# Two slots of 64 KB, x and u in one DMA each, and a tail of groups of 4, 2, 1 and 1 rows

## The chip, the cores and the metric

One NeuronCore of a Trainium2 chip runs the whole kernel. The metric is the device time of one execution in microseconds. The kernel before takes 653.01 us (median of three runs, 652.92 to 654.58).

## The reference

x is 8192 x 64, adj 8192 x 8192, u 8192 x 64, all float32.

```python
keep = (u >= 0.1).astype(x.dtype)
x_drop = x * keep / (1.0 - 0.1)
y = x + jnp.matmul(adj, x_drop)
out = (y - mean(y)) / sqrt(var(y) + 1e-5)     # over the 64 features of each row
```

adj has 268.4 MB, and each element of it is used once, against the 64 columns of x_drop.

## The kernel before

Row r of the output is row p * 64 + t, partition p, position t; a "row" of the kernel is one t, so it stands for 128 rows of the output. adj is rearranged on the host into chunks that are loaded as they lie. The output is made in groups: 7 full groups of R = 8 rows and short ones of 4, 2 and 2. For each group all 64 tiles of the contraction (KT) are multiplied: weights x_drop[:, t] (64 columns), moving data adj, the sum in PSUM `acc`. The lower half of the group's columns goes to partitions 0 to 63, the upper half to 64 to 127 (`product`, L168); a float32 product is two matmul passes in the trace, so a tile of a full group is 4 passes of 512 columns.

SP (L109) loads chunks of [128 x 8192] float32 (32 KB per partition, 4 MB) into a ring of four slots. It loads slot s again once `chunk_used` says that PE has done the chunk in it. The last chunk comes in five pieces (L124). ACT's queue (L155) loads x and u in four column pieces each; DVE (L259) waits for piece i of both and makes x_drop from it in two operations; PE waits for `drop_ready` before the tiles that need it. A chunk of a full group is 8 tiles, so two chunks use one piece.

At a group's end ACT copies acc to SBUF (L144), PE transposes it back (`turn_back`, L178), DVE adds x (L224), takes bn_stats per row (L230), combines the halves' statistics (L236 to L246), ACT takes the root (L147), DVE the reciprocal and the normalised rows (L252), and ACT's queue stores them (L152). PE goes on with the next group right after its transposes. The order on each engine is the program's; semaphores join them:

```python
with sp.Fori(1, CHUNKS // SLOTS - 1) as turn:
    for s in range(SLOTS):
        sp.wait_ge(chunk_used, (turn - 1) * SLOTS + s + 1)
        sp.dma_start(adj_ring[:, s, :], adj[turn * SLOTS + s]).then_inc(chunk_loaded[s], 16)
```

Of the kernel before, what the change touches and what calls it, by code (L numbers as in the profile page):

```python
# [26 lines left out]

assert FULL * R + sum(SHORT) == KT
assert sum(LAST_PARTS) == SLOT

SHORT_GROUPS = [(FULL * R + sum(SHORT[:n]), rows, FULL * NC + sum(SHORT[:n]) * NC // R)
                for n, rows in enumerate(SHORT)]


def build(nc: bass.Bass, x: bass.AP, adj: bass.AP, u: bass.AP, out: bass.AP):

# [11 lines left out]
    out_rows = out.rearrange("(p t) d -> p (t d)", p=P)  # L48

    with ExitStack() as ctx:  # L50
# [13 lines left out]
        identity = sb("identity", [P, P])  # L64
        eps = sb("eps", [P, 1])
# [25 lines left out]
        identity_ready = sem("identity_ready")  # L91
        acc_copied = sem("acc_copied")
# [10 lines left out]
        normed_ready = sem("normed_ready")  # L103
        out_stored = sem("out_stored")

        block = ctx.enter_context(nc.Block())

        @block.sync
        def _(sp):  # L109

            for s in range(SLOTS):
                sp.dma_start(adj_ring[:, s, :], adj[s]).then_inc(chunk_loaded[s], 16)
            with sp.Fori(1, CHUNKS // SLOTS - 1) as turn:
                for s in range(SLOTS):

                    sp.wait_ge(chunk_used, (turn - 1) * SLOTS + s + 1)
                    sp.dma_start(adj_ring[:, s, :], adj[turn * SLOTS + s]).then_inc(chunk_loaded[s], 16)  # L117

            first = CHUNKS - SLOTS
            for s in range(SLOTS - 1):  # L120
                sp.wait_ge(chunk_used, first - SLOTS + s + 1)
                sp.dma_start(adj_ring[:, s, :], adj[first + s]).then_inc(chunk_loaded[s], 16)
            sp.wait_ge(chunk_used, CHUNKS - SLOTS)
            for i, width in enumerate(LAST_PARTS):  # L124
                cols = slice(sum(LAST_PARTS[:i]), sum(LAST_PARTS[:i]) + width)
                sp.dma_start(adj_ring[:, SLOTS - 1, cols], adj[CHUNKS - 1][:, cols]).then_inc(last_loaded[i], 16)

# [7 lines left out]

        @block.scalar
        def _(act):
            def group(n, row, rows, chunks, parts):

                act.wait_ge(chunk_used, chunks)  # L140
                width = rows * P // 2 // parts
                for b in range(parts):

                    nc.scalar.copy(acc_sb[:, b * width:(b + 1) * width],  # L144
                                   acc[:, b * width:(b + 1) * width]).then_inc(acc_copied, 1)
                act.wait_ge(squares_ready, n + 1)
                nc.scalar.activation(std[:, 0:rows], squares[:, 0:rows], ACT.Sqrt, scale=1.0 / D,  # L147
                                     bias=eps[:]).then_inc(std_ready, 1)


                act.wait_ge(normed_ready, n + 1)
                act.dma_start(out_rows[:, bass.ds(row * D, rows * D)],  # L152
                              normed[:, bass.ds(row * D, rows * D)]).then_inc(out_stored, 16)

            for i in range(PIECES):  # L155
                cols = slice(i * PIECE, (i + 1) * PIECE)
                act.dma_start(x_nat[:, cols], x_rows[:, cols]).then_inc(x_loaded[i], 16)  # L157
                act.dma_start(u_nat[:, cols], u_rows[:, cols]).then_inc(x_loaded[i], 16)  # L158
            act.wait_ge(eps_ready, 1)
            with act.Fori(0, FULL) as g:  # L160
                group(g, g * R, R, (g + 1) * NC, 2)
            for n, (row, rows, chunk) in enumerate(SHORT_GROUPS):
                group(FULL + n, row, rows, chunk + rows * NC // R, 1)
            act.wait_ge(out_stored, 16 * (FULL + len(SHORT)))

        @block.tensor
        def _(pe):
            def product(rows, slot, tt, t):  # L168

# [19 lines left out]
            part_at = [sum(LAST_PARTS[:i]) for i in range(len(LAST_PARTS))]  # L189

            pe.wait_ge(identity_ready, 1)
            with pe.Fori(0, FULL) as g:
                tiles = SLOT // (R * P)
                for k in range(NC):
                    if k * tiles % PT == 0:
                        pe.wait_ge(drop_ready, k * tiles // PT + 1)

                    pe.wait_ge(chunk_loaded[k % SLOTS], (g * (NC // SLOTS) + k // SLOTS + 1) * 16)
                    for tt in range(tiles):
                        last = product(R, k % SLOTS, tt, k * tiles + tt)  # L200
                    last.then_inc(chunk_used, 1)
                turn_back(R, 2, g * 2)
            for n, (row, rows, chunk) in enumerate(SHORT_GROUPS):
                tiles = SLOT // (rows * P)
                for k in range(KT // tiles):
                    slot = (chunk + k) % SLOTS
                    final = chunk + k == CHUNKS - 1
                    if not final:
                        pe.wait_ge(chunk_loaded[slot], ((chunk + k) // SLOTS + 1) * 16)
                    for tt in range(tiles):  # L210
                        if final and tt * rows * P in part_at:
                            pe.wait_ge(last_loaded[part_at.index(tt * rows * P)], 16)
                        last = product(rows, slot, tt, k * tiles + tt)
                    last.then_inc(chunk_used, 1)
                turn_back(rows, 1, 2 * FULL + n)

        @block.vector
        def _(dve):
            def group(n, row, rows, parts, done):

                width = rows * D // parts
# [36 lines left out]

            for i in range(PIECES):  # L259
                cols = slice(i * PIECE, (i + 1) * PIECE)  # L260
                dve.wait_ge(x_loaded[i], 32)
                nc.vector.scalar_tensor_tensor(out=x_drop[:, cols], in0=u_nat[:, cols], scalar=P_DROP,  # L262
                                               in1=x_nat[:, cols], op0=ALU.is_ge, op1=ALU.mult
                                               ).then_inc(kept_ready, 1)
                dve.wait_ge(kept_ready, i + 1)
                nc.vector.tensor_scalar(x_drop[:, cols], x_drop[:, cols], 1.0 / (1.0 - P_DROP), None,  # L266
                                        ALU.mult).then_inc(drop_ready, 1)
            with dve.Fori(0, FULL) as g:
                group(g, g * R, R, 2, g * 2)
            for n, (row, rows, _) in enumerate(SHORT_GROUPS):  # L270
                group(FULL + n, row, rows, 1, 2 * FULL + n)
# [26 lines left out]
```

## Time and profile before

| | us |
|---|---|
| median of 3 runs | 653.01 |
| the profiled execution | 654.65 |
| its span, first to last instruction | 652.8 |
| PE busy | 493.9 (76%) |
| DVE busy | 45.5 |
| ACT busy | 26.4 |
| mean granted TensorE clock | 0.94 |

Busy times are sums over the span; the DMA lines say how many GB/s the core's 16 DMA engines moved in each of 40 equal slices. In a timeline a bracket holds the idle time of the engine before the line and what ended it. "DMA to landing" is the time from the issue of a transfer until it is complete.

### The profile page before, as it was taken

What the parts mean: (1) busy time and instruction counts of PE and PEld (TensorE: products, weight loads), DVE (VectorE), ACT (ScalarE), POOL (GpSimd) and SP (SyncE); (2) the same over time, 40 slices, a digit from 0 to 9 for tenths busy, and PEclk for the clock granted to TensorE, in tenths of its full rate; (3) what the DMA queues carried; (4) which work ended last, traced back from release to release, by engine and by line L of the source; (5) the groups of instructions that cost most, each with busy time, mean ns of one, the idle gap of its engine ahead of it and who ended that gap; (6) DMA issues with size and microseconds to landing.
All of it is one profiled execution on the core that took longest, in us unless ns stands there. A gap on an engine that the chain in (4) does not pass through costs nothing.

```text
span 652.8 us, 5964 instructions
## 1 busy us (share of the span) xinstructions
PE 493.9 (76%) x2592; PEld 189.4 (29%) x2592; DVE 45.5 (7%) x223; ACT 26.4 (4%) x41; POOL 0.7 (0%) x7
## 2 busy tenths in 40 slices
PE   0269569986987778886886777976878777976877
PEld 0023123322222222222222222222222222344776
DVE  0100111100020001000020000200002000020111
ACT  0000001000010001000010000200002000000000
POOL 0000000000000000000000000000000000000000
PEclk9998689999988989989989989999889989999889
DMA  8999999999999999999999999999999999999992
GB/s 357 434 434 432 434 416 443 432 424 442 426 432 428 442 420 444 432 424 442 426 430 430 440 422 442 424 434 438 430 430 437 432 420 444 424 429 438 434 409 99
DMA packets 12394, 274.87 MB, mean 421 GB/s; under 512 B 1377, under 2 KB 1761, under 8 KB 4065
## 3 DMA queue, kind: packets, MB, share of 16 engines
q1 hardware_dynamic: 9792, 268.44, 95.7%
q10 hardware_dynamic: 2592, 6.29, 2.5%
q8 instruction: 8, 0.13, 0.1%
q14 instruction: 2, 0.01, 0.0%
HBM read 272.63 MB, written 2.10 MB: 421 GB/s over the span
## 4 chain that ended last, share of the span: by engine, by line
DMA 68%; PE 23%; another core or an unknown queue 6%; DVE 1%; issue 1%; ACTq 0%; ACT 0%; SPq 0%; DVEq 0%
DMA adj_ring<-adj_chunks 61%; PE acc L173 22%; DMA u_nat<-u 7%; DVE x_drop L262 1%; DVE x_drop L266 0%; PE back L186 0%; SPq L117 0%; ACTq L157 0%; ACT acc_sb L144 0%; DVE u_nat L252 0%; ACTq L158 0%; DVE stats L230 0%; ACT std L147 0%; DVE summed L224 0%
## 5 line engine op out<-in xcount | busy, mean ns | idle before, releaser
L173 PE MATMUL acc<-adj_ring,x_drop 128*64 128x512 f32 (+2 forms) x2560 | 487.8, 540 | 149.9 <-DMA adj_ring<-adj_chunks 103.6
L173 PEld LDWEIGHTS acc<-adj_ring,x_drop 128*64 128x64 f32 x2560 | 186.1, 145 | 446.5 <-issue 320.4
L224 DVE TENSOR_TENSOR summed<-back,x_nat 128x256 f32<-128x256 f32 (+1 forms) x17 | 6.3, 405 | 512.8 <-PE back L186 512.8
L144 ACT COPY acc_sb<-acc 128x256 f32<-128x256 f32 (+1 forms) x17 | 5.4, 362 | 583.0 <-PE acc L173 583.0
L252 DVE TENSOR_SCALAR u_nat<-summed,mean,rstd 128x64 f32 (+1 forms) x64 | 15.2, 309 | 1.0
L262 DVE SCALAR_TENSOR_TENSOR x_drop<-u_nat,x_nat 128x1024 f32<-128x1024 f32 x4 | 4.9, 1225 | 87.2 <-DMA u_nat<-u 87.2
L144 ACT ACT_TABLE_LOAD x7 | 9.0, 1283 | 23.9 <-DVE u_nat L252 18.7
L186 PE MATMUL back<-identity,acc_sb 128*128 128x128 f32 x32 | 6.1, 302 | 4.5 <-ACT acc_sb L144 4.5
L230 DVE BATCH_NORM_STATS2 stats<-summed 128x6 f32<-128x64 f32 x64 | 9.0, 210 | 0.1
L147 ACT ACT_TABLE_LOAD x7 | 9.0, 1283 | 0.1
L186 PEld LDWEIGHTS back<-identity,acc_sb 128*128 128x128 f32 x32 | 3.3, 140 | 12.1 <-ACT acc_sb L144 11.6
L147 ACT ACTIVATE std<-squares,eps 128x8 f32<-128x8 f32 (+2 forms) x10 | 3.0, 300 | 16.6 <-DVE squares L246 16.6
L266 DVE TENSOR_SCALAR x_drop<-x_drop 128x1024 f32<-128x1024 f32 x4 | 2.8, 694 | 0.1
L249 DVE RECIPROCAL rstd<-std 128x8 f32<-128x8 f32 (+2 forms) x10 | 1.9, 193 | 3.7 <-ACT std L147 3.7
L236 DVE TENSOR_TENSOR gap<-stats 128x8 f32<-128x8 f32 (+2 forms) x10 | 1.7, 169 | 0.3
L244 DVE TENSOR_SCALAR mean<-twice_mean 128x8 f32<-128x8 f32 (+2 forms) x10 | 1.7, 171 | 0.0
L238 DVE TENSOR_TENSOR twice_mean<-stats 128x8 f32<-128x8 f32 (+2 forms) x10 | 1.6, 162 | 0.0
L237 DVE TENSOR_TENSOR within<-stats 128x8 f32<-128x8 f32 (+2 forms) x10 | 1.6, 162 | 0.0
L246 DVE TENSOR_TENSOR squares<-within,between 128x8 f32<-128x8 f32 (+2 forms) x10 | 1.6, 160 | 0.0
L240 DVE SCALAR_TENSOR_TENSOR between<-gap 128x8 f32<-128x8 f32 (+2 forms) x10 | 1.6, 158 | 0.0
L133 POOL TENSOR_SCALAR_AFFINE_SELECT identity<-identity 128x128 f32<-128x128 f32 x1 | 0.3, 295 | 0.2 <-POOL identity L131 0.2
L131 POOL MEMSET identity<- 128x128 f32 x1 | 0.2, 205 | 0.0
(5 smaller groups left out, 0.5 us busy)
## 6 DMA issues: line engine op xcount, KB each, us to landing
adj_ring<-adj_chunks SPq DMA_DIRECT2D x63, 4096.0 KB, 31.5
x_nat<-x ACTq DMA_DIRECT2D x4, 512.0 KB, 46.1
u_nat<-u ACTq DMA_DIRECT2D x4, 512.0 KB, 56.6
adj_ring<-adj_chunks SPq DMA_DIRECT2D x1, 2048.0 KB, 27.2
out<-u_nat ACTq DMA_DIRECT2D x7, 256.0 KB, 14.2
adj_ring<-adj_chunks SPq DMA_DIRECT2D x1, 1024.0 KB, 29.4
adj_ring<-adj_chunks SPq DMA_DIRECT2D x1, 512.0 KB, 30.2
adj_ring<-adj_chunks SPq DMA_DIRECT2D x2, 256.0 KB, 30.4
```

The source lines that it names most:

```text
L144: nc.scalar.copy(acc_sb[:, b * width:(b + 1) * width], acc[:, b * width:(b + 1) * width]).then_inc(acc_copied, 1)
L147: nc.scalar.activation(std[:, 0:rows], squares[:, 0:rows], ACT.Sqrt, scale=1.0 / D, bias=eps[:]).then_inc(std_ready, 1)
L173: last = nc.tensor.matmul(acc[h * D:(h + 1) * D, 0:width], x_drop[:, t * D:(t + 1) * D], adj_ring[:, slot, at:at + width], start=(t == 0), ...
L186: last = nc.tensor.transpose(back[b][:, c * P:(c + 1) * P], acc_sb[:, at:at + P], identity[:])
L224: nc.vector.tensor_tensor(summed[:, b * width:(b + 1) * width], back[b][:, 0:width], x_nat[:, bass.ds(row * D + b * width, width)], ALU.ad ...
L230: last = nc.vector.bn_stats(stats[:, r, :], summed[:, r * D:(r + 1) * D])
L236: nc.vector.tensor_tensor(gap[:, 0:rows], m0, m1, ALU.subtract).then_inc(gap_ready, 1)
L244: nc.vector.tensor_scalar(mean[:, 0:rows], twice_mean[:, 0:rows], 0.5, None, ALU.mult)
L249: nc.vector.reciprocal(rstd[:, 0:rows], std[:, 0:rows]).then_inc(rstd_ready, 1)
L252: last = nc.vector.tensor_scalar(normed[:, bass.ds((row + r) * D, D)], summed[:, r * D:(r + 1) * D], mean[:, r:r + 1], rstd[:, r:r + 1], A ...
L262: nc.vector.scalar_tensor_tensor(out=x_drop[:, cols], in0=u_nat[:, cols], scalar=P_DROP, in1=x_nat[:, cols], op0=ALU.is_ge, op1=ALU.mult). ...
L266: nc.vector.tensor_scalar(x_drop[:, cols], x_drop[:, cols], 1.0 / (1.0 - P_DROP), None, ALU.mult).then_inc(drop_ready, 1)
```

## The change

The main loop loads [128 x 16384] (64 KB per partition, 8 MB, 16 tiles) into two slots, and the seven full groups are 28 such chunks. x and u are loaded whole, by one DMA each; x_drop is still made in four parts. The short groups become 4, 2, 1 and 1 rows; their loads are pieces of 2 MB and 1 MB and, in the last group, of 16, 16, 8, 8, 6, 4, 3, 2 and 1 tiles of 64 KB. A group of one row has no second half: even tiles of the contraction add up in partitions 0 to 63 and odd ones in 64 to 127, and a product with `twofold` (two identities above one another) adds the two and turns them back. In the last group x is added by a product with the identity into PSUM tile `final`, and bn_stats, bn_aggr and the normalising work straight from PSUM. The tail's groups have PSUM tiles of their own, and their transposes stand behind the first piece of the next group. The copies out of PSUM move from ACT to DVE. The ring is one flat buffer, with one count `adj_used` of pieces done.

```diff
-SHORT = [4, 2, 2]
-SLOT = 8192
-SLOTS = 4
-LAST_PARTS = [4096, 2048, 1024, 512, 512]
+SLOT = 16384
+SLOTS = 2
+MAIN = FULL * NC
+RING = SLOTS * SLOT
+TAIL = [(4, [8] * 8), (2, [16, 16, 8, 8, 8, 8]), (1, [16] * 4), (1, [16, 16, 8, 8, 6, 4, 3, 2, 1])]
+WIDE = TAIL[0][1][0] * TAIL[0][0] * P
...
@@ sync
+            with sp.Fori(1, MAIN // SLOTS) as turn:
                 for s in range(SLOTS):
+                    sp.wait_ge(adj_used, (turn - 1) * SLOTS + s + 1)
+                    sp.dma_start(adj_ring[:, s * SLOT:(s + 1) * SLOT],
+                                 adj_main[turn * SLOTS + s]).then_inc(chunk_loaded[s], 16)
+            for i, (_, _, start, width, at) in enumerate(pieces(0)):
+                sp.wait_ge(adj_used, MAIN - SLOTS + at // SLOT + 1)
+                sp.dma_start(adj_ring[:, at:at + width], tail_block(start, width)).then_inc(piece_loaded[0][i], 16)
+            for n in range(1, len(TAIL)):
+                for i, (_, _, start, width, at) in enumerate(pieces(n)):
+                    sp.wait_ge(adj_used, MAIN + (at + width - 1) // WIDE + 1)
+                    sp.dma_start(adj_ring[:, at:at + width], tail_block(start, width)).then_inc(piece_loaded[n][i], 16)
@@ scalar
-            for i in range(PIECES):
-                cols = slice(i * PIECE, (i + 1) * PIECE)
-                act.dma_start(x_nat[:, cols], x_rows[:, cols]).then_inc(x_loaded[i], 16)
-                act.dma_start(u_nat[:, cols], u_rows[:, cols]).then_inc(x_loaded[i], 16)
+            act.dma_start(x_nat[:], x_rows).then_inc(x_loaded, 16)
+            act.dma_start(u_nat[:], u_rows).then_inc(x_loaded, 16)
@@ tensor
+            def product_of_one(into, at, t):
+                h = t % 2
+                return nc.tensor.matmul(into[h * D:(h + 1) * D, 0:P], x_drop[:, t * D:(t + 1) * D],
+                                        adj_ring[:, at:at + P], start=(t < 2), stop=(t >= KT - 2))
...
+                    if i == 0 and n in (1, 2):
+                        turn_back(TAIL[n - 1][0], 1, 2 * FULL + n - 1)
+                    if i == 0 and n == 3:
+                        pe.wait_ge(acc_copied, 2 * FULL + 3)
+                        pe.wait_ge(twofold_ready, 1)
+                        nc.tensor.matmul(back[0][:, 0:D], acc_sb[:, 0:P], twofold[:],
+                                         start=True, stop=True).then_inc(back_ready, 1)
+                    if i == 1 and n == 3:
+                        row = FIRST_ROW[LAST]
+                        nc.tensor.matmul(final[:], identity[:], x_nat[:, row * D:(row + 1) * D], start=True, stop=False)
+            pe.wait_ge(acc_copied, 2 * FULL + 4)
+            nc.tensor.matmul(final[:], acc_sb[:, 0:P], twofold[:], start=False, stop=True).then_inc(final_ready, 1)
@@ vector
+            def take(into, rows, used, parts):
+                dve.wait_ge(adj_used, used)
+                width = max(rows, 2) * P // 2 // parts
+                for b in range(parts):
+                    nc.vector.tensor_copy(acc_sb[:, b * width:(b + 1) * width],
+                                          into[:, b * width:(b + 1) * width]).then_inc(acc_copied, 1)
...
-                dve.wait_ge(x_loaded[i], 32)
+            dve.wait_ge(x_loaded, 32)
...
+            take(last_acc, 1, MAIN + FIRST_PIECE[LAST] + len(TAIL[LAST][1]), 1)
+            dve.wait_ge(final_ready, 1)
+            nc.vector.bn_stats(stats[:, 0, :], final[:]).then_inc(final_stats, 1)
+            dve.wait_ge(final_stats, 1)
+            nc.vector.bn_aggr(mean_var[:], stats[:, 0, :]).then_inc(final_var, 1)
+            dve.wait_ge(std_ready, FULL + LAST + 1)
+            nc.vector.reciprocal(rstd[:, 0:1], std[:, 0:1]).then_inc(rstd_ready, 1)
+            dve.wait_ge(rstd_ready, FULL + LAST + 1)
+            row = FIRST_ROW[LAST]
+            nc.vector.tensor_scalar(normed[:, row * D:(row + 1) * D], final[:], mean_var[:, 0:1], rstd[:, 0:1],
+                                    ALU.subtract, ALU.mult).then_inc(normed_ready, 1)
```

## Rows read from the trace of the kernel before

**Rows 1.** The page: the span, GB/s in 40 slices, DMA totals

```profile
span 652.8 us, 5964 instructions
...
GB/s 357 434 434 432 434 416 443 432 424 442 426 432 428 442 420 444 432 424 442 426 430 430 440 422 442 424 434 438 430 430 437 432 420 444 424 429 438 434 409 99
DMA packets 12394, 274.87 MB, mean 421 GB/s; under 512 B 1377, under 2 KB 1761, under 8 KB 4065
```

**Rows 2.** DMA queues of the page: packets, MB, share of 16 engines

```profile
q1 hardware_dynamic: 9792, 268.44, 95.7%
q10 hardware_dynamic: 2592, 6.29, 2.5%
```

**Rows 3.** Stretches: us, busy by engine, granted clock, DMA share, GB/s

```profile
0.00:5.00 5.00, 0.00 (x0) 0.00 (x0) 0.00 (x0) 0.00 (x0) 0.74 (x7) 1.00 0.66 223
...
5.00:605.00 600.00, 456.59 (x2038) 155.26 (x2040) 38.93 (x183) 24.59 (x35) 0.00 (x0) 0.94 1.00 431
...
50.00:55.00 5.00, 5.00 (x14) 1.31 (x15) 0.00 (x0) 0.00 (x0) 0.00 (x0) 0.50 0.91 385
...
640.00:642.00 2.00, 2.00 (x42) 2.00 (x40) 0.00 (x0) 0.00 (x0) 0.00 (x0) 1.00 0.24 92
```

**Rows 4.** Chain of waits: start us, us, what

```profile
364.98 31.45 DMA adj_ring<-adj_chunks
...
631.72 15.88 PE acc L173 x256
```

**Rows 5.** Lines L126 (last pieces' loads) and L152 (stores): duration ns, starts, landing

```profile
L126 SPq DMA_DIRECT2D adj_ring<-adj_chunks x5: 328/432/434, 609.4 to 611.2; - x5
...
DMA to landing us min/median/max: 27.2/30.2/30.5
...
DMA to landing us min/median/max: 1.6/14.2/15.4
```

**Rows 6.** Timeline of 0 to 100 us: start us, us, engine, line

```profile
25.77 1.23 DVE L262 SCALAR_TENSOR_TENSOR x_drop<-u_nat,x_nat 128x1024 f32<-128x1024 f32 x1 [25.77 <-DMA u_nat<-u]
...
27.87 15.70 PE L173 MATMUL acc<-adj_ring,x_drop 128*64 128x512 f32 x64 [27.87 <-DVE x_drop L266]
...
36.89 53.73 SPq L117 DMA_DIRECT2D adj_ring<-adj_chunks  x6
...
47.81 1.23 DVE L262 SCALAR_TENSOR_TENSOR x_drop<-u_nat,x_nat 128x1024 f32<-128x1024 f32 x1 [20.08 <-DMA u_nat<-u]
...
73.16 16.94 PE L173 MATMUL acc<-adj_ring,x_drop 128*64 128x512 f32 x64 [6.68 <-DVE x_drop L266]
...
93.07 1.22 DVE L262 SCALAR_TENSOR_TENSOR x_drop<-u_nat,x_nat 128x1024 f32<-128x1024 f32 x1 [20.04 <-DMA u_nat<-u]
```

**Rows 7.** Timeline of PE, 111 to 500 us

```profile
112.66 27.69 PE L173 MATMUL acc<-adj_ring,x_drop 128*64 128x512 f32 x128 [0.17 <-issue]
...
201.09 8.78 PE L173 MATMUL acc<-adj_ring,x_drop 128*64 128x512 f32 x32 [3.13 <-DMA adj_ring<-adj_chunks]
...
357.71 7.09 PE L173 MATMUL acc<-adj_ring,x_drop 128*64 128x512 f32 x32 [3.20 <-DMA adj_ring<-adj_chunks]
```

**Rows 8.** Timeline of the end, from 647 us

```profile
647.62 0.27 ACT L144 COPY acc_sb<-acc 128x128 f32<-128x128 f32 x1 [16.11 <-PE acc L173]
...
647.94 0.33 PE L186 MATMUL back<-identity,acc_sb 128*128 128x128 f32 x1 [0.36 <-ACT acc_sb L144]
...
648.70 0.35 DVE L230 BATCH_NORM_STATS2 stats<-summed 128x6 f32<-128x64 f32 x2
...
649.69 0.30 ACT L147 ACTIVATE std<-squares,eps 128x2 f32<-128x2 f32 x1 [1.80 <-DVE squares L246]
650.02 0.17 DVE L249 RECIPROCAL rstd<-std 128x2 f32<-128x2 f32 x1 [0.36 <-ACT std L147]
650.23 0.54 DVE L252 TENSOR_SCALAR u_nat<-summed,mean,rstd 128x64 f32<-128x64 f32 x2
650.80 0.35 ACTq L152 DMA_DIRECT2D out<-u_nat  x1
```

More of the change, by code:

```diff
@@ L16, with pieces @@
 FULL = 7
-SHORT = [4, 2, 2]
-SLOT = 8192
-SLOTS = 4
-CHUNKS = KT * KT * P // SLOT
+SLOT = 16384
+SLOTS = 2
 NC = KT * R * P // SLOT
-LAST_PARTS = [4096, 2048, 1024, 512, 512]
-PIECES = 4
-PT = KT // PIECES
-PIECE = PT * D
-HALF = R * P // 2
[L28 to L32, printed above, removed]
+MAIN = FULL * NC
+RING = SLOTS * SLOT
+TAIL = [(4, [8] * 8), (2, [16, 16, 8, 8, 8, 8]), (1, [16] * 4), (1, [16, 16, 8, 8, 6, 4, 3, 2, 1])]
+FIRST_ROW = [FULL * R + sum(rows for rows, _ in TAIL[:n]) for n in range(len(TAIL))]
+FIRST_PIECE = [sum(len(tiles) for _, tiles in TAIL[:n]) for n in range(len(TAIL))]
+WIDE = TAIL[0][1][0] * TAIL[0][0] * P
+X_PARTS = 4
+PART = KT * D // X_PARTS
+PT = KT // X_PARTS
+HALF = R * P // 2
+assert FULL * R + sum(rows for rows, _ in TAIL) == KT
+assert all(sum(tiles) == KT for _, tiles in TAIL)
+assert MAIN % SLOTS == 0 and len(TAIL[0][1]) * WIDE == RING
+def pieces(n):
+    rows, tiles = TAIL[n]
+    at = sum(TAIL[m][0] for m in range(n)) * KT * P
+    out = []
+    for i, count in enumerate(tiles):
+        before = sum(tiles[:i])
+        out.append((before, count, at + before * rows * P, count * rows * P, (at + before * rows * P) % RING))
+    return out
 def build(nc: bass.Bass, x: bass.AP, adj: bass.AP, u: bass.AP, out: bass.AP):
@@ L48, in build, with tail_block @@
     out_rows = out.rearrange("(p t) d -> p (t d)", p=P)
+    adj_main = adj[0:MAIN * P * SLOT].rearrange("(n p c) -> n p c", p=P, c=SLOT)
+    def tail_block(start, width):
+        first = (MAIN * SLOT + start) * P
+        return adj[first:first + width * P].rearrange("(p c) -> p c", p=P)
     with ExitStack() as ctx:
@@ L64, in build @@
         identity = sb("identity", [P, P])
+        twofold = sb("twofold", [P, D])
         eps = sb("eps", [P, 1])
@@ L111, in _ @@
             for s in range(SLOTS):
-                sp.dma_start(adj_ring[:, s, :], adj[s]).then_inc(chunk_loaded[s], 16)
-            with sp.Fori(1, CHUNKS // SLOTS - 1) as turn:
+                sp.dma_start(adj_ring[:, s * SLOT:(s + 1) * SLOT], adj_main[s]).then_inc(chunk_loaded[s], 16)
+            with sp.Fori(1, MAIN // SLOTS) as turn:
                 for s in range(SLOTS):
[L116 to L126, printed above, removed]
+                    sp.wait_ge(adj_used, (turn - 1) * SLOTS + s + 1)
[8 more added lines that the diff above has]
+                    sp.dma_start(adj_ring[:, at:at + width], tail_block(start, width)).then_inc(piece_loaded[n][i], 16)
         @block.gpsimd
@@ L134, in _, with root @@
                                     base=0, pattern=[[-1, P]], channel_multiplier=1).then_inc(identity_ready, 1)
+            pool.wait_ge(identity_ready, 1)
+            nc.gpsimd.tensor_tensor(twofold[:], identity[:, 0:D], identity[:, D:P], ALU.add).then_inc(twofold_ready, 1)
         @block.scalar
         def _(act):
[L138 to L145, printed above, removed]
+            def root(n, rows):
                 act.wait_ge(squares_ready, n + 1)
@@ L148, in group, with store @@
                                      bias=eps[:]).then_inc(std_ready, 1)
+            def store(n, row, rows):
                 act.wait_ge(normed_ready, n + 1)
@@ L196, in _ @@
                         pe.wait_ge(drop_ready, k * tiles // PT + 1)
[L198 removed]
+                    s = k % SLOTS
+                    pe.wait_ge(chunk_loaded[s], (g * (NC // SLOTS) + k // SLOTS + 1) * 16)
                     for tt in range(tiles):
[L200 to L201 removed]
+                        last = product(acc, R, s * SLOT + tt * R * P, k * tiles + tt)
@@ L202, in _ @@
+                    last.then_inc(adj_used, 1)
                 turn_back(R, 2, g * 2)
[L203 to L215, printed above, removed]
+            for n, (rows, _) in enumerate(TAIL):
+                into = tail_acc[n] if n < LAST else last_acc
+                for i, (before, count, _, _, at) in enumerate(pieces(n)):
+                    pe.wait_ge(piece_loaded[n][i], 16)
+                    for tt in range(count):
+                        if rows > 1:
+                            last = product(into, rows, at + tt * rows * P, before + tt)
+                        else:
+                            last = product_of_one(into, at + tt * P, before + tt)
+                    last.then_inc(adj_used, 1)
+                    if i == 0 and n in (1, 2):
[8 more added lines that the diff above has]
+                        nc.tensor.matmul(final[:], identity[:], x_nat[:, row * D:(row + 1) * D], start=True, stop=False)
@@ L221, in group, with normalise @@
+            def normalise(n, row, rows, parts, done):
                 width = rows * D // parts
@@ L256, in group @@
                 dve.wait_ge(normed_ready, n + 1)
-            for i in range(PIECES):
-                cols = slice(i * PIECE, (i + 1) * PIECE)
-                dve.wait_ge(x_loaded[i], 32)
+            dve.wait_ge(x_loaded, 32)
+            for i in range(X_PARTS):
+                cols = slice(i * PART, (i + 1) * PART)
                 nc.vector.scalar_tensor_tensor(out=x_drop[:, cols], in0=u_nat[:, cols], scalar=P_DROP,
@@ L268, in _ @@
             with dve.Fori(0, FULL) as g:
-                group(g, g * R, R, 2, g * 2)
-            for n, (row, rows, _) in enumerate(SHORT_GROUPS):
-                group(FULL + n, row, rows, 1, 2 * FULL + n)
+                take(acc, R, (g + 1) * NC, 2)
+                normalise(g, g * R, R, 2, g * 2)
+            for n in range(LAST):
+                take(tail_acc[n], TAIL[n][0], MAIN + FIRST_PIECE[n] + len(TAIL[n][1]), 1)
+                normalise(FULL + n, FIRST_ROW[n], TAIL[n][0], 1, 2 * FULL + n)
+            take(last_acc, 1, MAIN + FIRST_PIECE[LAST] + len(TAIL[LAST][1]), 1)
[9 more added lines that the diff above has]
+                                    ALU.subtract, ALU.mult).then_inc(normed_ready, 1)
 def kernel(x, adj, L0_gnn_u):
@@ L279 @@
     x, adj, u = np.asarray(x), np.asarray(adj), np.asarray(L0_gnn_u)
-    chunks = np.empty((CHUNKS, P, SLOT), adj.dtype)
-    by_row = adj.reshape(P, KT, N)
-    groups = [(g * R, R, g * NC) for g in range(FULL)] + SHORT_GROUPS
-    for row, rows, first in groups:
-        tiles = SLOT // (rows * P)
-        n = KT // tiles
-        part = by_row[:, row:row + rows].reshape(P, rows // 2, 2, P, n, tiles).transpose(4, 3, 5, 2, 1, 0)
-        chunks[first:first + n].reshape(n, P, tiles, 2, rows // 2, P)[...] = part
-    arrays = {"x": x, "adj_chunks": chunks, "u": u}
+    by_row = adj.reshape(P, KT, P, KT)
+    blocks = np.empty(N * N, adj.dtype)
+    tiles = SLOT // (R * P)
+    for g in range(FULL):
+        part = by_row[:, g * R:(g + 1) * R].reshape(P, R // 2, 2, P, NC, tiles).transpose(4, 3, 5, 2, 1, 0)
+        blocks[g * NC * P * SLOT:(g + 1) * NC * P * SLOT].reshape(part.shape)[...] = part
+    for n, (rows, _) in enumerate(TAIL):
+        h = 2 if rows > 1 else 1
+        group = by_row[:, FIRST_ROW[n]:FIRST_ROW[n] + rows].reshape(P, rows // h, h, P, KT).transpose(3, 4, 2, 1, 0)
+        for before, count, start, width, _ in pieces(n):
+            first = (MAIN * SLOT + start) * P
+            part = group[:, before:before + count]
+            blocks[first:first + width * P].reshape(part.shape)[...] = part
+    arrays = {"x": x, "adj_blocks": blocks, "u": u}
     nc = bacc.Bacc("TRN2", target_bir_lowering=False, num_devices=1)
```

46 lines of the change are left out of this document (30 added, 16 removed).

## The prediction

> **What bounds the kernel now.** I read the page first. The cores' 16 DMA engines move 431 to 433 GB/s in nearly every slice, from the second to the last but one, and between 5 and 605 us the mean is 431 GB/s with the engines' share at 1.00, while PE has idle time [rows 1, 3]. Almost all bytes are adj on SP's queue; x, u and the output are 6.3 MB on ACT's queue [rows 2]. So the kernel is a stream of 274.9 MB with two ends: before it flows, and after it stops. The chain of waits, read second, says the same: it goes round a loop of one 4 MB load, 31.45 us from issue to landing, and one chunk's products, 7.09 us [rows 4, 7]. Four slots at 38.8 us a loop are 9.7 us a chunk, and 4.19 MB at 431 GB/s are 9.73 us: the loop runs at the stream's pace, and most of the 31.45 us is waiting behind other loads, a reserve. Whatever leaves the DMA engines without a queued load is lost for good; whatever only PE, DVE or ACT do inside the stream is free. Third, the stretches at the end: the stream is nearly out in 640 to 642 us (92 GB/s) [rows 3], the last piece, issued at about 611.2, lands 30.2 us later, at 641.4 [rows 5], but PE works until 647.6, because the last group's 256 matmul passes run as one block from 631.72 [rows 4]; then come copy, transpose, sum, statistics, root and store, and the span ends at 652.8 [rows 8]. The end is 11.4 us behind the last landing.
>
> **Part 1, x and u in one DMA each, beside two slots of 64 KB.** Here I expect the loss. How do ACT's and SP's queues share an engine? The page counts 9792 packets on q1 [rows 2]: 63 loads with 128 rows of 32 KB, the last chunk's 5 x 128, and 68 DMAs x 16 small ones, which makes 9792 exactly, so one partition's row is one packet. The pieces of x and u have rows of 4 KB, 8 of x and 8 of u on each of 16 engines. DVE starts on the first piece at 25.77 and on the second at 47.81; there are four, evenly spaced, to 93.07 [rows 6]. If the two queues take turns packet by packet, 16 turns of 32 + 4 KB on 16 engines are 9.44 MB, at 431 GB/s 21.9 us; the rows show 22.0. By bytes in equal shares it would have been 1.05 MB of x, u and as much of adj, 4.9 us. Turns it is.
>
> Afterwards a row of x is 16 KB, a row of adj 64 KB, and there are 8 + 8 rows of either per engine before anything can be freed: the two slots hold 16 rows of 64 KB per engine. 16 turns of 80 KB on 16 engines are 20.97 MB, which is the whole ring and all of x and u. So x and u are complete only when there is nothing left to load. In time: the first 5 us carry 223 GB/s, 1.1 MB [rows 3]; the other 19.86 MB need 46.1 us; the engines run dry at 51.1. For the check, the same working gives 24.3 us for the present first piece, and DVE started at 25.77, so 1.5 us lie between last byte and use: 52.6. From DVE's start to PE's first matmul are 2.1 us (27.87 - 25.77), since x_drop still comes in quarters [rows 6]: 54.7. The first slot is 16 tiles, 64 passes of 512 columns. Before, just such blocks took 15.70 to 16.94 us after a long rest [rows 6]; I take 15.7: 70.4. Only then does SP refill slot 0. Issue to first byte isn't shown by itself: it is above 0, and below the 1.6 us in which the shortest store is issued and landed [rows 5]. I take 0.8 with SP's wait: data flow at 71.3. **The DMA engines stand idle for 20.2 us** (18.7 to 22.5 with the bounds). Before, the ring of four was first refilled at 36.89 [rows 6], while 16.8 MB of adj weren't in yet, and never ran dry. The fewer DMA instructions on ACT's queue (8 become 2) save nothing on this path. Nothing gives it back, as the stream is the bound to the end.
>
> **Part 2, the steady loop of two slots.** A slot's round is: its products, SP's wake and issue, the load. 8.39 MB are 19.46 us, so a round may last 38.9. Products: 14.0 us at full clock, 2.4 GHz (128 passes back to back took 27.69), and a start at 1.2 GHz costs 8.78 against 7.09 for 4 MB, 1.7 us more; both kinds follow rests of 3.1 to 3.2 us [rows 7]. (In 50 to 55 us, after a rest of 6 us, the granted clock is 0.50 [rows 3].) PE would now rest 19.46 - 15.7, some 3.7 us, so I take the slow start, 15.7 us, with 14.0 and 16.94 as ends. Wake and release are 0.2. What a load takes beyond its bytes is between 1.6 us (the shortest store whole) and 3.1 (1.5 of landing plus the 1.6). Sums: 14.0 + 0.2 + 19.46 + 1.6 = 35.3 at best, 16.94 + 0.2 + 19.46 + 3.1 = 39.7 at worst, in the middle 37.7. So it fits by about 1.2 us where there were some 20 us in reserve. The 13 further rounds cost 0 to 13 x 0.8 = 10 us; I take 1 us, for the first ones, which follow long rests. The evacuation at a group's end, now on DVE, and the transposes (0.8 us of copies, 0.7 of PE, by the nearest rows) begin after the slot is given back, in PE's rest of some 3.7 us; at no cost, and uncovered 1.5 us a group. DVE's next group is 78 us away. The ACT table loads that fall away are off the path.
>
> The Trainium skill ("DMA: Bandwidth & Descriptors", 🔬 Anatomy of one DMA) puts a DMA's fixed cost at about 2.0 us beside its bytes at 436 GB/s, mostly completion. As an estimate from that page a round would be 15.7 + 0.2 + 19.3 + 2.0 = 37.2 us, and the loop would hold too; no row here isolates it.
>
> **Part 3, the tail.** SP's tail loads wait only for regions whose products run earlier, up to 16.8 MB ahead, so they stay queued. In bytes nothing changes. More and shorter rows (down to 512 B; before, 2 KB was the shortest of adj) cost the stream 0 to 1 us; I take 0.3. The gain is that the last landing leaves one tile: two passes and what is left of the tile pairs before. PE's pace is enough: a row's 64 tiles are 128 passes of 128 columns in 9.7 us, while before 256 such passes took 15.88 [rows 4], 7.9 per 128. I take 0.4 us from the last landing to PE's end (0.2 if it is waiting, 3 if it meets the end at half clock with a piece behind), against 6.2. Then the chain: before, 647.60 to the store's issue at 650.80 is 3.2 us. Now: a copy on DVE of 128 columns (nearest row: ACT's 0.27; 0.2 to 0.3, take 0.25), one product of 64 columns (0.33 for the 128 column transpose, take 0.30), one bn_stats (0.21 by the two in 0.35), bn_aggr (not shown; 0.16 to 0.30, take 0.2), root 0.30, reciprocal 0.17, one tensor_scalar out of PSUM (0.54 for two, take 0.27) and 8 hand-overs of 0.04 as seen in the rows: 2.0 us [rows 8]. Store to the end 2.0 as before (652.8 - 650.8). So the end is 4.4 us behind the last landing instead of 11.4: **7.0 us won** (4 to 7.5).
>
> **The sum**, on the profiled execution (span 652.8, time 654.65): 20.2 + 1.0 + 0.3 - 7.0 = +14.5 us, so span 667.3 and time 669.2. The median of the runs shown, 653.01, lies 1.6 under the profiled one, so I forecast 667.5.
>
> **Rivals.**
> A. *x and u land early.* Mechanism: ACT's queue gets a larger share beside rows of 64 KB, in equal bytes or because a long row goes in two packets of 32 KB. Place: the first 50 us. The point that decides: DMA stays busy if u lands before 51.1 - 2.1 - 15.7 - 0.8 = 32.5 us. In equal bytes 8.4 MB are due, and u is in by 5 + 16.9 + 1.5 = 23.4; with 32 KB packets 16 turns of 48 KB, 12.6 MB, and in at 33.1: idle 0.6 us. Then the time is 653.0 + 0 to 0.6 + 1.3 - 7.0 = 647.3 to 648, with a bad loop up to 655. For it: no row of 64 KB is in the trace. Against it: 32 KB rows went whole, and the spacing of 22.0 us rules out equal bytes at that size. Chance 0.12. The Trainium skill ("DMA: Bandwidth & Descriptors", 🔬 SWDGE vs HWDGE vs iDMA) calls a packet of at most 4096 B, preferably, the boundary where an engine switches; by that rule this rival would hold. The trace disagrees with it for this queue: 22.0 us, not 4.9.
>
> B. *The loop of two starves.* PE at half clock for longer, or engines that finish a load unevenly, with nothing behind them: 0.3 to 0.8 us a chunk, 26 chunks, 8 to 20 us on top of the forecast: 675 to 687. For it: 1.2 us of reserve, and blocks of 16.94 us. Against it: a starved loop gives PE no more work, and the present rate stays within 431 to 433. Chance 0.13.
>
> C. *The tail doesn't shorten* (PE ends behind the last piece as before, by the many small matmuls and weights): 3 to 6 us more, 671 to 674. Chance 0.08.
>
> **Chances and range.** Forecast 0.67, A 0.12, B 0.13, C 0.08. From A at 647 to 655: faster 0.09, same 0.02, slower 0.01; all others are slower. Beyond 0.3% (2 us, about what can be told from no change): faster 0.09, same 0.03, slower 0.88. The range 662 to 678 leaves out A and the upper part of B.
>
> **What would show it.** In the page's slices: a hole in the DMA row of some 20 us near 51 to 71 us and none before it; DVE's first x_drop near 52.6; SP's third load issued near 70.4. In 100 to 560 us: 431 GB/s and loads of about 23 us from issue to landing; a mean under 427 means B. At the end: PE finished within 0.5 us of the last landing, and 4.4 us to the end. The forecast is wrong if DVE starts before 33 us, or if the queue share of ACT's rows isn't one row a turn.

## The result: 685.2 us, slower by 4.7%

| | us | ratio to before | 95% interval |
|---|---|---|---|
| before (4 runs beside it) | 653.80 | | |
| changed | 685.23 (680.8 to 685.99) | 1.0467 | 1.0418 to 1.0515 |

The forecast was 667.5 us with a range of 662 to 678: the sign was right, the loss 31.4 us instead of 14.5, and the time lies above the range. The profiled execution took 685.4 us, its span 683.6. Executions of the kernel before fall near 653.1 or near 654.7 us, which is why its median differs a little from one set of runs to another (653.01 and 653.80, and 653.06 to 653.16 in the experiments).

In what follows PE is the matmul engine, DVE the vector engine, ACT the scalar engine; SP's and ACT's queues issue the transfers, and all of them are carried by the same 16 DMA engines. The trace has a record for each row (one partition's part of a transfer) with its start and duration; figures said to be from the rows' records come from there.

The slices of the page after, as in [rows 1], the DMA row ahead of GB/s:

```profile
DMA  9990899999999999999999999999999999999996
GB/s 374 454 399 0 369 429 427 429 433 406 403 429 385 428 426 433 429 432 404 410 418 429 440 404 410 426 414 399 426 429 426 430 402 422 402 415 402 424 420 244
DMA packets 9801, 274.87 MB, mean 402 GB/s; under 512 B 1344, under 2 KB 1984, under 8 KB 3392
```

Two things are to be seen: a slice of 17 us in which nothing at all moves, and then a stream that keeps falling to 385 to 415, where before hardly a slice was under 420. The bytes are the same. The start, from the timelines of DVE, PE and SP after (answering to [rows 6]):

```profile
52.02 1.23 DVE L303 SCALAR_TENSOR_TENSOR x_drop<-u_nat,x_nat 128x1024 f32<-128x1024 f32 x1 [52.02 <-DMA u_nat<-u]
...
54.12 29.98 PE L197 MATMUL acc<-adj_ring,x_drop 128*64 128x512 f32 x128 [54.12 <-DVE x_drop L307]
...
70.56 502.07 SPq L142 DMA_DIRECT2D adj_ring<-adj_blocks  x26
```

Forecast were 52.6, 54.7 and 70.4. In the rows' records the last data of x, u and the first two slots end at 51.4 us and the next row of adj starts at 71.5: a hole of 20.1 us, where 20.2 were forecast. The records show the turns too. From 4.9 us on, 16 rows of ACT's queue start, one for each engine, then 16 of SP's, sixteen times over, 3.0 us a turn. The queues' packets between 10.8 and 13.8 us (q1 is SP's, q10 ACT's):

```profile
q1 hardware_dynamic: 16, 1.05, 80.6%
q10 hardware_dynamic: 16, 0.26, 20.4%
```

This excludes a rival that the times of u alone leave open: if the queues took turns load by load, eight rows an engine at once, u would be in at the same time.

The stretches (columns as in [rows 3]) show the hole, and then the loop:

```profile
50.00:70.00 20.00, 15.88 (x64) 5.21 (x66) 7.40 (x8) 0.00 (x0) 0.00 (x0) 1.00 0.03 13
...
100.00:560.00 460.00, 365.12 (x1482) 121.36 (x1480) 31.30 (x162) 9.50 (x12) 0.00 (x0) 0.88 0.99 420
```

420 GB/s over 460 us instead of 431 to 432. The engines' busy share is 0.99 all the same. The chain of waits goes round this loop (as [rows 4], two slots now):

```profile
314.67 15.66 PE acc L197 x64
330.36 0.05 SPq L142
330.50 23.82 DMA adj_ring<-adj_blocks
...
394.80 16.59 PE acc L197 x64
411.40 0.05 SPq L142
411.55 23.43 DMA adj_ring<-adj_blocks
```

A load's median from issue to landing is 24.2 us, the median block of products 15.7. The end, answering to [rows 8]:

```profile
675.69 3.71 PE L205 MATMUL tail_acc<-adj_ring,x_drop 128*64 128x128 f32 x64
679.54 0.29 DVE L259 COPY acc_sb<-tail_acc 128x128 f32<-128x128 f32 x1 [4.35 <-PE tail_acc L205]
...
679.89 0.43 PE L251 MATMUL final<-twofold,acc_sb 128*128 128x64 f32 x2 [0.49 <-DVE acc_sb L259]
680.36 0.23 DVE L318 BATCH_NORM_STATS2 stats<-final 128x6 f32<-128x64 f32 x1 [0.53 <-PE final L251]
680.63 0.18 DVE L320 BATCH_NORM_AGGREGATE mean_var<-stats 128x2 f32<-128x6 f32 x1
680.84 0.29 ACT L187 ACTIVATE std<-mean_var,eps 128x1 f32<-128x1 f32 x1 [6.20 <-DVE mean_var L320]
...
681.37 0.34 DVE L325 TENSOR_SCALAR u_nat<-final,mean_var,rstd 128x64 f32<-128x64 f32 x1
681.75 0.35 ACTq L174 DMA_DIRECT2D out<-u_nat  x1
```

The tail has 27 loads; the last is issued at 663.3 and lands 15.2 us later, at 678.5. From there PE takes 0.9 us, the chain 2.35 to the store's issue, the store 1.85 to the end of the span: 5.1 us, where it was 11.4.

### The profile page after: what moved, and what is told of

The parts are those of the page before. It is cut to its first block, busy times and chain, and to the rows that moved or that the text cites. A ratio compares the mean times of both kernels' runs of the same rounds, so it can differ in the third digit from the quotient of the medians.

```text
span 683.6 us, 5863 instructions
## 1 busy us (share of the span) xinstructions
PE 508.5 (74%) x2597; PEld 196.1 (29%) x2597; DVE 52.3 (8%) x243; ACT 12.3 (2%) x18; POOL 1.1 (0%) x8
## 4 chain that ended last, share of the span: by engine, by line
DMA 54%; PE 37%; another core or an unknown queue 8%; DVE 1%; issue 1%; SPq 0%; ACT 0%; DVEq 0%
DMA adj_ring<-adj_blocks 54%; PE acc L197 35%; PE tail_acc L197 1%; PE tail_acc L205 1%; DVE x_drop L303 0%; SPq L142 0%; PE back L213 0%; DVE acc_sb L259 0%; DVE x_drop L307 0%; PE final L251 0%; PE final L249 0%; DVE u_nat L325 0%; ACT std L187 0%; DVE stats L318 0%
## 5 line engine op out<-in xcount | busy, mean ns | idle before, releaser
L197 PE MATMUL acc<-adj_ring,x_drop 128*64 128x512 f32 x1792 | 443.0, 658 | 161.7 <-DMA adj_ring<-adj_blocks 107.6
L197 PEld LDWEIGHTS acc<-adj_ring,x_drop 128*64 128x64 f32 x1792 | 146.1, 151 | 453.9 <-issue 398.4
L197 PE MATMUL tail_acc<-adj_ring,x_drop 128*64 128x256 f32 (+1 forms) x512 | 42.9, 327 | 3.3 <-DMA adj_ring<-adj_blocks 3.3
L259 DVE COPY acc_sb<-acc 128x256 f32<-128x256 f32 x14 | 5.3, 419 | 516.5 <-PE acc L197 516.5
L197 PEld LDWEIGHTS tail_acc<-adj_ring,x_drop 128*64 128x64 f32 x512 | 32.1, 137 | 14.1 <-DMA adj_ring<-adj_blocks 5.0
L205 PE MATMUL tail_acc<-adj_ring,x_drop 128*64 128x128 f32 x256 | 15.5, 275 | 2.7 <-DMA adj_ring<-adj_blocks 2.7
L205 PEld LDWEIGHTS tail_acc<-adj_ring,x_drop 128*64 128x64 f32 x256 | 13.8, 137 | 4.0 <-DMA adj_ring<-adj_blocks 4.0
L169 ACT ACTIVATE std<-squares,eps 128x8 f32<-128x8 f32 (+3 forms) x10 | 3.0, 299 | 642.3 <-DVE squares L288 642.3
L266 DVE TENSOR_TENSOR summed<-back,x_nat 128x256 f32<-128x256 f32 (+2 forms) x17 | 6.2, 400 | 12.1 <-PE back L213 9.5
L291 DVE RECIPROCAL rstd<-std 128x8 f32<-128x8 f32 (+3 forms) x10 | 1.9, 193 | 3.7 <-ACT std L169 3.7
L278 DVE TENSOR_TENSOR gap<-stats 128x8 f32<-128x8 f32 (+3 forms) x10 | 1.7, 169 | 0.3
## 6 DMA issues: line engine op xcount, KB each, us to landing
adj_ring<-adj_blocks SPq DMA_DIRECT2D x28, 24.2
adj_ring<-adj_blocks SPq DMA_DIRECT2D x1, 384.0 KB, 22.2
```

Of the source, the lines that this page charges most:

```text
L197: last = nc.tensor.matmul(into[h * D:(h + 1) * D, 0:width], x_drop[:, t * D:(t + 1) * D], adj_ring[:, at + h * width:at + (h + 1) * width] ...
L205: return nc.tensor.matmul(into[h * D:(h + 1) * D, 0:P], x_drop[:, t * D:(t + 1) * D], adj_ring[:, at:at + P], start=(t < 2), stop=(t >= KT ...
L259: nc.vector.tensor_copy(acc_sb[:, b * width:(b + 1) * width], into[:, b * width:(b + 1) * width]).then_inc(acc_copied, 1)
L266: nc.vector.tensor_tensor(summed[:, b * width:(b + 1) * width], back[b][:, 0:width], x_nat[:, bass.ds(row * D + b * width, width)], ALU.ad ...
L278: nc.vector.tensor_tensor(gap[:, 0:rows], m0, m1, ALU.subtract).then_inc(gap_ready, 1)
L291: nc.vector.reciprocal(rstd[:, 0:rows], std[:, 0:rows]).then_inc(rstd_ready, 1)
```

## The experiments

Each ratio is to the kernel before on the same chip.

### 1. Four slots of 32 KB, the rest as changed

```diff
-SLOT = 16384
-SLOTS = 2
+SLOT = 8192
+SLOTS = 4
```

> The changed kernel with its main loop put back to four slots of 32 KB rows; x and u stay in one DMA each, the tail stays. My theory: all of the loss is in the two slots, 20 us at the start and 16 to 17 us in the loop, and the tail gains. Taking turns row by row, u is in after 16 turns of 48 KB, near 33 us, the ring isn't dry before 51, so no hole in the DMA row; 431 GB/s in 100 to 560 us; time 653.8 - 7 + 1.2 = 648 us. Rival (the new tail or the single DMAs lose by themselves): 655 us or more, with a hole before 60 us or an end as long as before.

Measured: 649.51 us, ratio 0.9945 (0.9928 to 0.9961); run again beside experiment 10: 649.55, 0.9944 (0.9930 to 0.9958). Its timelines and stretch:

```profile
33.14 1.23 DVE L303 SCALAR_TENSOR_TENSOR x_drop<-u_nat,x_nat 128x1024 f32<-128x1024 f32 x1 [33.14 <-DMA u_nat<-u]
...
43.85 487.42 SPq L142 DMA_DIRECT2D adj_ring<-adj_blocks  x52
...
100.00:560.00 460.00, 361.94 (x1522) 117.49 (x1524) 31.08 (x162) 9.50 (x12) 0.00 (x0) 0.94 1.00 432
```

DVE starts at the forecast 33, no slice is empty, the rate is 432. So the whole loss of the change, 35.7 us beside this kernel, comes with the size and number of the slots, and the new tail is a gain: 3.6 us, less than the 5.8 expected here.

### 2. Slot 1's first load behind x and u

```diff
-            for s in range(SLOTS):
-                sp.dma_start(adj_ring[:, s * SLOT:(s + 1) * SLOT], adj_main[s]).then_inc(chunk_loaded[s], 16)
+            sp.dma_start(adj_ring[:, 0:SLOT], adj_main[0]).then_inc(chunk_loaded[0], 16)
...
             act.dma_start(u_nat[:], u_rows).then_inc(x_loaded, 16)
+            act.dma_start(adj_ring[:, SLOT:2 * SLOT], adj_main[1]).then_inc(chunk_loaded[1], 16)
```

> The changed kernel, with the first load of slot 1 issued on ACT's queue behind x and u instead of on SP's queue. If the queues take turns row by row, SP's queue has only 8 rows per engine beside x and u, so u is in after 12.6 MB, near 33 us, PE starts near 35 and gives slot 0 back near 51, when the ring is just dry: the hole of 20 us shrinks to under 2 us, and the time is 685 - 19.6 = 665.6 us. If the shares go by something else (bytes, or a priority of SP's queue), the start moves little and the time stays above 675.

Measured: 665.28 us, 1.0207 (1.0159 to 1.0254). Same slots, same bytes, another order of two loads:

```profile
32.39 1.22 DVE L303 SCALAR_TENSOR_TENSOR x_drop<-u_nat,x_nat 128x1024 f32<-128x1024 f32 x1 [32.39 <-DMA u_nat<-u]
...
50.37 504.39 SPq L141 DMA_DIRECT2D adj_ring<-adj_blocks  x26
...
50.00:70.00 20.00, 14.14 (x66) 5.41 (x64) 0.00 (x0) 0.00 (x0) 0.00 (x0) 0.97 1.00 417
100.00:560.00 460.00, 366.43 (x1490) 121.59 (x1488) 31.34 (x162) 9.50 (x12) 0.00 (x0) 0.89 0.99 419
```

The hole is gone and 20.0 us are back in the median (four runs, 663.6 to 670.4); the loop is as slow as it was. The start's loss is shown by itself.

### 3. x and u in four pieces beside slots of 64 KB

```diff
-            act.dma_start(x_nat[:], x_rows).then_inc(x_loaded, 16)
-            act.dma_start(u_nat[:], u_rows).then_inc(x_loaded, 16)
+            for i in range(X_PARTS):
+                cols = slice(i * PART, (i + 1) * PART)
+                act.dma_start(x_nat[:, cols], x_rows[:, cols]).then_inc(x_loaded[i], 16)
+                act.dma_start(u_nat[:, cols], u_rows[:, cols]).then_inc(x_loaded[i], 16)
```

> The changed kernel with x and u in four column pieces each, as before; slots of 64 KB stay. Theory of turns (a row a turn): the first pieces still need 16 turns, now of 64 + 4 KB, 17.8 MB, so DVE starts near 45 us instead of 52, PE near 47.4, slot 0 is given back near 63, and only 7 us come back: 685.2 - 7 = 678 us. Rival (it is the single DMA of x and u that makes the hole, as the change's text would have it): DVE starts near 26, no hole, 665 us.

Measured: 674.42 us, 1.0302 (1.0266 to 1.0337). DVE starts at 45.14 (forecast 45), SP refills at 63.50 (63). The turns hold again; the time is 3.6 us better than worked out, within the 5 us by which runs of a two-slot loop differ among themselves (670.5 to 675.9 here).

### 4. The kernel before with x and u in one DMA each

The same edit the other way round, in the kernel before.

> The kernel before with x and u in one DMA each and nothing else changed: 16 turns of 32 + 16 KB, u in near 33 us, PE's first chunk done near 44, ring dry only at 51, so no hole and the same time as before, 653 us within 0.3%. If the single DMA costs by itself, 655 us or more.

Measured: 652.68 us, 0.9986 (0.9975 to 0.9997): the same within 0.3%. DVE starts at 33.55, PE at 35.65, SP refills at 44.25. The single DMAs cost nothing; the 16 rows of 64 KB per engine beside them do.

### 5. Rows of 32 KB in slots of 64 KB

```diff
-                sp.dma_start(adj_ring[:, s * SLOT:(s + 1) * SLOT], adj_main[s]).then_inc(chunk_loaded[s], 16)
+                for h in range(2):
+                    sp.dma_start(adj_ring[:, s * SLOT + h * SLOT // 2:s * SLOT + (h + 1) * SLOT // 2],
+                                 adj_main[s][:, h * SLOT // 2:(h + 1) * SLOT // 2]).then_inc(chunk_loaded[s], 16)
```

(and in the loop likewise, with PE waiting for 32 a turn)

> The changed kernel, each slot of 64 KB loaded by two DMAs with rows of 32 KB; a slot is still released whole. Theory R (the loop loses because a slot is given back too late, only some 1 to 2 us before the other is in): the mean in 100 to 560 us stays near 418 GB/s; the start is mended by the shorter rows (u in near 33 us, idle under 2 us), so 685 - 19.6 = 666 us. Theory P (rows of 64 KB themselves make the loop slow): 431 GB/s and about 649 us.

Measured: 668.85 us (663.74 to 670.22), 1.0248 (1.0228 to 1.0268).

```profile
100.00:560.00 460.00, 364.88 (x1498) 121.91 (x1496) 31.34 (x162) 9.50 (x12) 0.00 (x0) 0.89 0.99 421
```

Theory R, as far as the rate goes: rows of 32 KB don't mend the loop. The traced execution is the fastest of the four, and the median lies 2.9 us above the forecast of 666.

### 6 and 7. Fewer products per slot

```diff
-                    for tt in range(tiles):
+                    for tt in range(0, tiles, 2):
```

This is experiment 6; experiment 7 has `range(tiles - 2)`. In both, the `stop` of the sum moves to the last product that is left. Both kernels leave out products and so don't compute the reference; they serve to time the loop.

> The changed kernel without the products of every second tile in the main loop, so the sum of the seven full groups is incomplete; a slot is given back after some 8 us instead of 16, loads unchanged. At the start the hole shrinks by 7.8 us either way. Theory R (late release): 431 GB/s in 100 to 560 us, 685 - 7.8 - 16.5 = 661 us. Theory P (rows of 64 KB are slow by themselves): near 418 GB/s and 677 us.

> The changed kernel without the products of the last two of each slot's 16 tiles in the main loop (the sum of the seven full groups is incomplete): a slot is given back some 2 us earlier, with about 6 us instead of 4 to the other slot's landing. Start: 2 us less. Theory of late release with a threshold of some 5 us: the loop is back at 431 GB/s, so 685.2 - 2 - 16 = 667 us. If each microsecond of PE's work counted in proportion (8 us less gave 12 GB/s): near 423 GB/s, 679 us.

Measured: with half of them 661.59 us, 1.0130 (1.0113 to 1.0147); with 14 of 16 tiles 668.94 us, 1.0234 (1.0217 to 1.0251). The stretches, first of half, then of 14 tiles:

```profile
100.00:560.00 460.00, 222.16 (x772) 69.45 (x774) 31.34 (x162) 9.50 (x12) 0.00 (x0) 0.72 1.00 432
```

```profile
100.00:560.00 460.00, 341.43 (x1338) 110.66 (x1334) 31.34 (x162) 9.50 (x12) 0.00 (x0) 0.85 1.00 432
```

With rows of 64 KB and two slots untouched, two tiles fewer bring back the full rate, and leaving out six more changes nothing further. There is a threshold. It isn't PE's work as such that slows the loads: with four slots PE does all the products and the rate is 432 (experiment 1). The threshold is read off PE's timeline, where the bracket, PE's rest, is the time from handing a slot back (and issuing its load) to the landing of the other slot. Three turns of the changed kernel, then three with 14 tiles:

```profile
476.53 16.66 PE L197 MATMUL acc<-adj_ring,x_drop 128*64 128x512 f32 x64 [6.03 <-DMA adj_ring<-adj_blocks]
496.32 15.31 PE L197 MATMUL acc<-adj_ring,x_drop 128*64 128x512 f32 x64 [3.13 <-DMA adj_ring<-adj_blocks]
516.17 15.63 PE L197 MATMUL acc<-adj_ring,x_drop 128*64 128x512 f32 x64 [4.53 <-DMA adj_ring<-adj_blocks]
```

```profile
130.11 15.15 PE L197 MATMUL acc<-adj_ring,x_drop 128*64 128x512 f32 x56 [3.48 <-DMA adj_ring<-adj_blocks]
150.04 13.72 PE L197 MATMUL acc<-adj_ring,x_drop 128*64 128x512 f32 x56 [4.79 <-DMA adj_ring<-adj_blocks]
169.41 14.28 PE L197 MATMUL acc<-adj_ring,x_drop 128*64 128x512 f32 x56 [5.64 <-DMA adj_ring<-adj_blocks]
```

Where a group ends, the transposes stand inside the rest, so it is longer than the bracket: at 130.11 it is 4.8 us in all. The distance of two starts is here that of two landings. Over 24 turns of the 14-tile kernel: after a rest of 4.5 us or less (5 turns) the load issued before it lands 20.0 to 20.5 us after the other one, after 4.7 us or more (19 turns) in 19.2 to 19.5, with one of 19.9. The pace of the full stream is 8.39 MB at 432 GB/s, 19.4. In the changed kernel the median rest is 4.2 us and the landings are 20.1 us apart in the mean, up to 22.3 and 21.5 after the shortest rests of 2.8 and 3.0. So the 14-tile kernel keeps the stream full if a load is issued some 4.7 us before the other one lands. In the changed kernel the single turns scatter more (six with a rest of 4.6 us or more are followed by 19.6 to 20.1), so 4.7 us is a figure of about that size, and not a sharp limit for every loop.

### 8. Eight slots of 16 KB

As experiment 1, with SLOT = 4096 and SLOTS = 8.

> The changed kernel with eight slots of 16 KB rows in the main loop, the same 128 KB ring. 16 turns of 32 KB: u in near 23.4 us, no hole, 431 GB/s; PE's rests fall to about 1.3 us, so the granted clock rises over 0.95, off the path. Time as with four slots, 649.5 us. If more and shorter loads cost by themselves, 651 us or more.

Measured: 653.35 us, 0.9999 (0.9989 to 1.0008). The forecast of 649.5 missed; the alternative named, 651 or more, came.

```profile
23.05 1.23 DVE L303 SCALAR_TENSOR_TENSOR x_drop<-u_nat,x_nat 128x1024 f32<-128x1024 f32 x1 [23.05 <-DMA u_nat<-u]
...
100.00:560.00 460.00, 344.99 (x1516) 103.41 (x1512) 28.25 (x145) 9.50 (x12) 0.00 (x0) 1.00 1.01 429
```

The start is as worked out (23.4), and with rests of some 1.2 us the granted clock is 1.00, which helps nothing. The rate is 429 with the engines' share at 1.01: rows of 16 KB move more slowly at full load. The rows' records say it of the single row: one of 16 KB takes 614 ns, one of 32 KB (experiment 1) 1216 and one of 64 KB (the changed kernel) 2418, in the median, which is 26.7, 26.95 and 27.1 GB/s for an engine. As an estimate from the rounded rates, 235 MB of the main loop at 429 instead of 432 GB/s are 3.8 us, about the whole difference to four slots.

### 9 and 10. Longer loads in the tail

```diff
-TAIL = [(4, [8] * 8), (2, [16, 16, 8, 8, 8, 8]), (1, [16] * 4), (1, [16, 16, 8, 8, 6, 4, 3, 2, 1])]
+TAIL = [(4, [16] * 4), (2, [32, 32]), (1, [32, 32]), (1, [16, 16, 8, 8, 6, 4, 3, 2, 1])]
-                    if i == 1 and n == 3:
+                    if i == 0 and n == 3:
```

> Four slots of 32 KB rows with the new tail, its loads made longer: groups of 4 and 2 rows in rows of 32 KB (4 x 16 tiles, 2 x 32 tiles), the first group of one row in 2 x 32 tiles; and the product that adds x to the last row moved one piece earlier. If short rows are what slows the stream in the tail (431 GB/s at 32 KB, 421 in 600 to 620 us with 8 KB), 25 MB at 431 instead of some 425 save 0.9 us and the product 0.4: 648.2 us, 1.3 under the four slots with the short pieces. Rival: the rate falls for another reason (the end of the ring, the stores), and nothing changes: 649.5.

> The kernel with four slots of 32 KB rows and the new tail once more, beside the one with the longer loads, for the difference of the two: 649.5 us.

Measured: 650.37 us, 0.9961 (0.9947 to 0.9975), against 649.55, 0.9944. The stretch from 600 us of the long loads, then of the short ones:

```profile
600.00:620.00 20.00, 14.90 (x176) 12.29 (x178) 0.42 (x1) 0.00 (x0) 0.00 (x0) 0.91 1.00 428
```

```profile
600.00:620.00 20.00, 16.37 (x242) 13.66 (x240) 3.20 (x17) 0.30 (x1) 0.00 (x0) 1.00 1.00 420
```

The stream did get faster, 428 against 420, and its last load lands at 642.2 instead of 642.5. But PE, which now gets 4 MB at a time, falls behind: in the long version it hardly rests from 621.93 on and ends at 644.26, 1.0 us later than in the short one (643.28). The gain expected in the stream was lost to PE's lag; neither the forecast of 648.2 nor the rival's 649.5 came.

## Why the prediction was wrong, step by step

**The start was right.** The step "16 turns of 64 + 16 KB, so x and u are in only when nothing is left to load" gave 20.2 us; undoing it by itself gave back 20.0 (experiment 2). Three sizes of row put DVE's first operation at 23.05, 33.14 and 52.02 us, worked out as 23.4, 33.1 and 52.6. Rival A is refuted with it. The hole itself was 20.1 us against 20.2. (The bounds that the prediction names for PE's block and for the issue give 19.4 to 22.2 and not 18.7 to 22.5; the measured value lies in both.) The Trainium skill's packet of preferably at most 4096 B ("DMA: Bandwidth & Descriptors", 🔬 SWDGE vs HWDGE vs iDMA) stands there in a table on transfers issued by GpSimd; as a rule for these queues it would give one time for all three, and the runs show it isn't one: on SP's and ACT's queues the turn is a row, up to 64 KB.

**The steady loop failed, in one term.** The step was "What a load takes beyond its bytes is between 1.6 us and 3.1", from which "it fits by about 1.2 us", and 1 us of loss was taken. At the stream's pace a round of 38.9 us has room for 38.9 - 15.8 - 0.2 - 19.4 = 3.5 us between the issue of a load and the landing of the other one; I held 1.6 to 3.1 us to be enough, and experiment 7 shows that it takes about 4.7. In the changed kernel a load takes 24.2 us (median) from issue to landing, 4.8 beyond its 19.4 us of bytes. With the products' 15.8 (mean, forecast 15.7) and 0.2 a round is 40.2 us for two loads, 20.1 each, 0.7 above the pace. 25 such steps are 17.5 us; between experiments 2 and 1, 15.8 us went with it.

The time is that of rival B (675 to 687), which had 0.13; its price of 0.3 to 0.8 us a chunk was right, and I put it beside the forecast instead of in it. Its mechanism is half right. PE at half clock for longer was not it: the blocks of products were as long as forecast. Engines that finish a load unevenly are part of it, as the rows' records below show.

The upper bound was at fault: it was pieced together from the idle first load and the idle last store, and no row of before shows a load issued while another is in flight with little queued behind it. The shortest load seen, 22.2 us in all, even lies inside my bounds, so it is the pace, not the shortest time, that the 4.7 us decide. The Trainium skill's fixed cost of about 2.0 us ("DMA: Bandwidth & Descriptors", 🔬 Anatomy of one DMA), which the page gives for transfers issued by GpSimd, is less than half of it; here the measurement decides. (At the page's 436 GB/s the bytes are 19.2 us and not 19.3, so the prediction's estimate from it would be 37.1 us.)

**The tail gained 5.0 us in the spans of the profiled executions (652.8 to 647.8), not 6.7, and 3.6 in the medians.** The traced execution of before is one of those near 654.7 us and most of its others are near 653.1, so 3.6 us is what the tail is worth between typical executions. The stream's end came 1.3 us later (642.7 with four slots, against 641.4) instead of 0.3, as short rows run at 420 to 421 GB/s; PE's end is 0.8 us behind the last landing instead of 0.4; the chain after it takes 2.35 us instead of 2.0, since the copy and the product hand over at 0.35 and 0.47 us and the last two DVE operations read PSUM or follow ACT. Rival C did not come: PE kept up with the pieces.

**The sum again**, in spans: 652.8 + 20.0 + 15.8 - 5.0 = 683.6, the measured one. It closes because its terms are differences between the runs; what tests two of them apart from the total are the hole of 20.1 us in the rows' records and 0.7 us a load.

**Where the 0.7 us a load go.** The engines' share falls only from 1.00 to 0.99 while GB/s fall by 3%, so more than half of the loss isn't idle time but rows that take longer. The rows' records of the changed kernel's loop put about 0.3 us a load down to engines without a row and about 0.4 to rows above the usual 2.42 us; two thirds of the latter are in the first row that each engine moves of a load. That row is slow when it starts soon after the issue: within 1.5 us of it, it takes 3.1 us in the mean (97 rows), from 1.5 to 4 us 2.6 (275), later 2.42 (44). In the two kernels with fewer products it is the same, 3.1 to 3.2 us (28 rows) against 2.42 (542). And the 16 engines don't finish a load together: the first is done 1.3 to 3.7 us before the last, so it needs the next load that much earlier than the landing.

Not settled: what an engine does in those first 4 us, whether it is the fetching of a load's descriptors or something else. No run here was made for it.

## What to carry to other kernels

For a stream-bound kernel, ask of every ring how long before the engines run dry a load can be issued: the same 128 KB gave some 22 us of lead in four slots (31.5 from issue to landing, 9.7 of them the load's own bytes) and 4.2 in two, and about 4.7 were needed. When two queues share the DMA engines, count rows, not bytes: a small input beside long rows arrives after as many long rows as it has rows itself, counted on each engine. Four slots of 32 KB with the new tail, at 649.5 us, beat both kernels; finer slots lost what they won through shorter rows, and larger tail loads through PE.

## What the runs showed of the hardware that I had not expected

A load of 8 MB had to be issued about 4.7 us before the other one landed, against 1.6 us for a small store from issue to landing [rows 5].

The stream's rate depends on the row, at a DMA share of 1.00 or more: 432 GB/s with rows of 64 and of 32 KB, 429 with 16 KB, and 420 to 421 in 600 to 620 us of the tail, where half of the bytes are in rows of 16 KB and half in rows of 8 KB. In the rows' records there a row of 8 KB takes 311 ns, 26.3 GB/s for an engine.

SP was held up by its own issues in the tail. The line after, for the last 19 of the tail's 27 loads, as in [rows 5]:

```profile
L152 SPq DMA_DIRECT2D adj_ring<-adj_blocks x19: 327/2101/6581, 617.4 to 663.3; - x19
...
DMA to landing us min/median/max: 15.2/27.9/31.7
```

The median issue took 2.1 us and the longest 6.6 (11.2 with four slots), against 0.33 in the main loop. It isn't seen to cost anything: with four slots the engines' share is 1.00 in 600 to 620 us, as loads are queued ahead.
